# Half of the sums by source started while the rows are still being scattered

## The chip, the cores and the metric

One core of a Trainium2 chip runs the whole program. The metric is the device time of one execution in microseconds (us). The engines are PE (matrix products), DVE (vector), ACT (scalar), POOL (GpSimd, here it issues the indirect DMAs) and SP (SyncE, here it issues the plain DMAs). Each has its own queue and works through it in order; they wait for one another on semaphores.

## What is computed

Four graph layers over 3125 nodes of 128 features and 53125 edges sorted by destination. The part around the change is the first layer's sum of edge features by source and by destination:

```python
h = relu(layernorm(x))
edge_aggr = zeros(3125, 128)
edge_aggr = edge_aggr.at[row].add(edge_attr).at[col].add(edge_attr)   # row: source, col: destination
x = x + relu(concat([h, edge_aggr]) @ W1 + b1) @ W2 + b2
```

Layer 1 uses the sum by destination, layer 2 is a graph convolution over the same edges, layer 3 computes messages for each edge. All of them come after the stages told here.

## The kernel before

The edges are taken as 416 columns of 128 (EC). Four columns are a group (KC = 4, 104 groups), two are a pair (208 pairs, PG = 2 pairs a group). The nodes are 25 blocks of 128 (NB); source block b has its own region of 18 columns of rows in a DRAM table `rows_by_block` (CAP = 18 x 128 rows, the last block 9 columns), 129 words a row: the features and the node's number within its block.

**Scatter stage** (`place_and_count`). For each group g, PE computes with small matmuls the rank of every edge within its source block (`rank`, L895 to L905). DVE multiplies it with the block one-hots (`own_rank`, L834), reduces it to a place (L839) and casts it (L843); ACT copies the running count of each block as the base for the next group (`base_of_next`, L793). POOL then issues four indirect DMAs, each of which scatters one column of rows to its places (L769). SP loads the edge rows into a ring of eight groups. ACT writes the keys beside them (L779) and makes the low one-hots (`lows`, L786 and L789); DVE makes the wide one-hots (`hots`, L814 and L821), PE multiplies each pair (L921 to L930: a count of pairs of nodes, the sum by destination and the in-degree, into one of three PSUM bank pairs), and DVE adds the result to its window in SBUF (`collect`, L853 and L855), two pairs later. `rank` of group g+1 stands on PE ahead of the even pair of group g, and DVE's `which_block` (L828) for group g+2 waits for it, since the block one-hots are kept twice. Before each pair PE multiplies ones by ones (`stream_ones`, L384), three times, or 16 times in one of 32 pairs.

The order of each queue is the order of these loops. On ACT it is, for pair i: `lows(i)`, at the even pair the keys, at the odd pair `base_of_next(g+1)`, which waits for `own_rank(g+1)`. On DVE at the odd pair: `hots(i)`, `collect(i-2)`, `own_rank(g+1)`. On PE at the even pair: ones, `rank(g+1)`, pair; at the odd pair: ones, pair.

**Block sums** (`sum_blocks`). The table is read back block by block, in 74 reads of up to six columns (LR = 6) into four buffers (LB_IN = 4). DVE compares the keys of a read with 0 to 127 (L1125), PE sums the rows by these one-hots (L1181, float32: two matmul records for each column), and DVE adds the sum by destination (`add_dst`, L1117). Beside it ACT checks the counts of all 25 blocks in `between` (L1164), and DVE takes mean and variance of x. A small block then computes the flags that choose the fast path, and ends with 12 ones-matmuls; the dense layers follow.

Of the kernel before, what the change touches and what calls it, by code (L numbers as in the profile page):

```python
# [12 lines left out]
F32 = mybir.dt.float32  # L13
# [10 lines left out]
P = 128  # L24
# [57 lines left out]
LAST_BANK = 7  # L82
WARM_EVERY = 32


class Signal:
# [6 lines left out]
    def __init__(self, make, everywhere=False):  # L93
        self.make, self.everywhere, self.on_path, self.base = make, everywhere, {}, {}

    @property
    def h(self):
        branch = Signal.path is not None and not self.everywhere
        if branch not in self.on_path:
            self.on_path[branch] = self.make()  # L100
        return self.on_path[branch]
# [44 lines left out]
def build(nc, x, src, dst, ea, l0, l1, l2, l3, out):  # L146
    ctx = ExitStack()
    with ctx:
# [7 lines left out]
        def signal(name, everywhere=False):  # L156
# [3 lines left out]
            return Signal(make, everywhere)  # L160
# [98 lines left out]
        bounds = sb("bounds", [1, 2, NB])  # L259
        over = sb("over", [1, 2, NB])  # L260
# [22 lines left out]
        tab_row = sb("tab_row", [1, 2, 2, ST * P], I32)  # L283
        tab_bc = sb("tab_bc", [P, 2, 2, ST * P])

        shifts = [sb(f"shift{k}", [P, SLOTS_OF[k], GS[k]]) for k in range(2)]
# [15 lines left out]
        junk = grid_space.take([P, NP], U8)  # L302
        excess = grid_space.take([P, NB])
# [349 lines left out]
        pair_done = signal("pair_done")  # L653
        taken = signal("taken")
# [68 lines left out]
        def place_and_count():  # L723
# [15 lines left out]
            with nc.Block(no_gpsimd_drain=True) as block:  # L739
                @on(block.sync)  # L740
                def _(sp):
                    for g in range(ROWG, GROUPS):
# [6 lines left out]
                        if g == 6 * ROWG:  # L749
                            sp.wait_ge(vec.h, vec.at(1))  # L750
                            sp.dma_start(x_nm[:, 0:NB - 1, :], x[0:(NB - 1) * P, :].rearrange("(b p) f -> p b f", p=P)).then_inc(loaded.h, 16)
                            sp.dma_start(x_nm[0:NLAST, NB - 1, :], x[(NB - 1) * P:N, :]).then_inc(loaded.h, 16)
                    sp.wait_ge(loaded.h, loaded.at(16 * 23))
# [19 lines left out]
                def _(act):  # L773
# [24 lines left out]
                    for i in range(PAIRS):  # L798
# [4 lines left out]
                        if i % PG == 1 and g + 1 < GROUPS:  # L803
                            base_of_next(g + 1)

                @on(block.vector)
                def _(dve):
# [50 lines left out]

                    which_block(0)
                    which_block(1)  # L860
                    own_rank(0)
                    for i in range(PAIRS + 2):
# [11 lines left out]
                        if i % PG == 1 and g + 1 < GROUPS:  # L874
                            own_rank(g + 1)
# [1842 lines left out]
```

## Time and profile before

| | us |
|---|---|
| median of 3 runs (lowest to highest) | 1446.84 (1445.1 to 1453.07) |
| the profiled execution, its own time | 1445.09 |
| its span in the trace | 1443.2 |
| granted TensorE clock, mean | 0.971 of 2.4 GHz |
| scatter stage, first scatter to the first read of the block sums | 26.15 to 559.2 |
| block sums | 559.2 to 686 |

Times within the trace are counted from the start of the span. The profiled execution's own time is 1.9 us above its span. A busy time is that of instructions in work; what an engine waited for stands in brackets behind a row of the timeline.

### The profile page before, as it was taken

The numbers are of one execution on the slowest core, as the hardware profiler recorded it, in microseconds if no ns is written. First come the engines' busy times: TensorE is split into PE (matmuls) and PEld (weight loads), VectorE is DVE, ScalarE is ACT, GpSimd is POOL, SyncE is SP. The second block draws the span as 40 slices with busy tenths as digits, with TensorE's granted clock in tenths as the row PEclk, the third lists the DMA queues.
The fourth block names the chain that finished last, engine by engine and source line by source line (L and its number), as shares of the span: only waits on it lengthen the run. The fifth ranks groups of instructions, "written<-read, shape, count | busy, mean of one in ns | idle before, by whom it ended". The sixth has DMA issues, their size and how long they took to land. (4 is left out here: it accounts for less than half of the span.)

```text
span 1443.2 us, 32570 instructions
## 1 busy us (share of the span) xinstructions
PE 1243.0 (86%) x9643; PEld 908.2 (63%) x9644; DVE 881.1 (61%) x2785; ACT 555.4 (38%) x1465; POOL 809.5 (56%) x844
## 2 busy tenths in 40 slices
PE   5887888888888887898679998999999988898896
PEld 3554555555555555888459997477766766666665
DVE  6777878787877876766676537344444444444343
ACT  5444444444454446960222103333332222222222
POOL 5777777777777773000000000777777777777774
PEclk9999999999999999999889998899999999999997
DMA  7533335333333324877600001745555565555641
GB/s 230 137 106 104 104 105 148 102 105 104 106 104 106 107 72 138 237 246 217 30 18 2 2 1 52 203 133 153 156 154 155 161 159 150 152 140 145 149 111 42
DMA packets 198603, 174.73 MB, mean 121 GB/s; under 512 B 48820, under 2 KB 171174, under 8 KB 198342
## 3 DMA queue, kind: packets, MB, share of 16 engines
q1 hardware_dynamic: 171848, 118.36, 31.1%
q0 software_dynamic: 26624, 54.79, 12.9%
q8 instruction: 62, 1.02, 0.3%
q14 instruction: 69, 0.57, 0.2%
HBM read 134.89 MB, written 38.16 MB: 120 GB/s over the span
## 5 line engine op out<-in xcount | busy, mean ns | idle before, releaser
L2192 POOL DMA_INDIRECT between<-p_table,src_g x416 | 397.5, 956 | 472.5 <-DMA p_table<-n_nm 346.0
L384 PE MATMUL acc<-ones_b 128*128 128x512 bf16 x1603 | 425.5, 386 | 29.3 <-PEq L1407 15.5
L769 POOL DMA_INDIRECT rows_by_block<-h_t,mean_bc x312 | 300.6, 963 | 109.5 <-issue 77.1
L384 PEld LDWEIGHTS acc<-ones_b 128*128 128x128 bf16 x1603 | 142.5, 99 | 130.9 <-issue 39.2
L921 PE MATMUL acc<-n_nm 128*128 128x384 bf16 (+1 forms) x832 | 140.8, 291 | 87.2 <-DVE n_nm L821 86.4
L2302 ACT ACTIVATE between<-acc 128x256 f32<-128x256 f32 x208 | 79.9, 384 | 352.4 <-PE acc L2359 339.3
L853 DVE TENSOR_TENSOR between<-between,acc 128x600 f32 x208 | 161.3, 775 | 61.3 <-issue 51.7
L2391 PE MATMUL acc<-w_msg,between 128*128 128x128 f32 x832 | 184.1, 303 | 0.0
L2370 PEld LDWEIGHTS acc<-between 128*128 128x128 f32 x832 | 128.9, 197 | 71.4 <-issue 52.2
L2229 DVE TENSOR_TENSOR between<-acc,between 128x256 f32<-128x256 f32 x208 | 87.6, 421 | 139.9 <-DMA between<-p_table,src_g 90.0
L921 PEld LDWEIGHTS acc<-n_nm 128*128 128x128 bf16 x832 | 66.3, 97 | 164.0 <-DVE n_nm L821 134.8
L2370 PE MATMUL acc<-between 128*128 128x24 f32 x832 | 132.5, 240 | 42.4 <-DVE agg_sum L2269 40.7
L821 DVE TENSOR_SCALAR n_nm<-iota_w,agg_sum 128x600 bf16<-128x600 f16 x416 | 154.5, 412 | 0.0
L786 ACT ACTIVATE away<-iota_b,agg_sum 128x128 bf16<-128x128 bf16 x416 | 140.9, 385 | 0.0
L2391 PEld LDWEIGHTS acc<-w_msg,between 128*128 128x128 f32 x832 | 126.0, 191 | 1.7 <-issue 0.3
L793 ACT ACTIVATE bases<-acc 1x26 f32<-1x26 f32 x104 | 19.0, 182 | 265.7 <-DVE agg_sum L834 265.7
L1181 PE MATMUL acc<-n_nm,h_t 128*128 128x128 f32 x882 | 109.4, 280 | 11.5 <-DVE n_nm L1125 10.9
L769 POOL DMA_INDIRECT rows_by_block<-agg_sum,mean_bc x104 | 99.7, 959 | 32.5 <-issue 25.5
L2359 PE MATMUL acc<-ident,between 128*128 128x128 f32 x416 | 114.1, 275 | 0.0
L1181 PEld LDWEIGHTS acc<-n_nm,h_t 128*128 128x128 f32 x882 | 102.2, 191 | 18.8 <-DVE n_nm L1125 18.1
L789 ACT ACTIVATE n_nm<-away,ones 128x256 bf16<-128x256 bf16 x208 | 105.6, 508 | 6.8
L2269 DVE TENSOR_TENSOR agg_sum<-agg_sum,acc 128x24 f32 x208 | 37.4, 180 | 115.3 <-PE acc L2370 65.5
(204 smaller groups left out, 1950.4 us busy)
## 6 DMA issues: line engine op xcount, KB each, us to landing
h_t<-rows_by_block SPq DMA_DIRECT2D x73, 387.0 KB, 3.8
between<-in_edge_attr SPq DMA_DIRECT2D x207, 128.0 KB
h_t<-in_edge_attr SPq DMA_DIRECT2D x78, 256.0 KB, 3.2
between<-in_dst SPq DMA_DIRECT2D x51, 288.0 KB
between<-p_table,src_g POOLq DMA_INDIRECT x416
agg_sum<-in_edge_attr SPq DMA_DIRECT2D x25, 256.0 KB
rows_by_block<-h_t,mean_bc POOLq DMA_INDIRECT x312
rows_by_block<-x_nm SPq DMA_DIRECT2D x1, 4644.0 KB, 18.6
```

Source lines behind the costliest of these rows:

```text
L384: pe.matmul(acc[:, bank * BANK:(bank + 1) * BANK].rearrange("p (a n) -> p a n", n=P), ones_b[:, :], ones_b[:, :].rearrange("p (a n) -> p a ...
L769: pool.indirect_dma_start(rows_by_block, bass.IndirectOffsetOnAxis(ap=place_in_table[:, t:t + 1], axis=0), row_group(g)[:, j, :], None).th ...
L786: act.activation(away[:, h + j, :], iota_b[:, :], ACT.Abs, scale=-1.0, bias=lo_s[:, 2 * i + j:2 * i + j + 1])\
L789: act.activation(low_hot[:, h:h + 2, :], away[:, h:h + 2, :], ACT.Relu, scale=-1.0, bias=ones[:, 0:1]).then_inc(lows_made.h, 1)
L821: ins = dve.tensor_scalar(wide_hot[:, i % HOTB * 2 + j, :], iota_w[:, :], key_w[:, t:t + 1], None, ALU.is_equal)
L853: dve.tensor_tensor(between[:, :, bass.ds(first, W)], between[:, :, bass.ds(first, W)], acc[:, o:o + NB * WS].rearrange("p (b w) -> p b w" ...
L921: pe.matmul(acc[:, to:to + (b1 - b0) * WS].rearrange("p (b w) -> p b w", w=WS)[:, :, 0:W], low_hot[:, h + j, :], wide_hot[:, h + j, b0 * W ...
L1181: last = pe.matmul(acc[:, o:o + P], rows_in_block[:, q, j, 0:D], hot_in_block[:, q, j, :], start=is_first and j == 0, stop=is_last and j = ...
L2192: pool.indirect_dma_start(got[:, q, j * D:(j + 1) * D], None, p_table, bass.IndirectOffsetOnAxis(ap=src_g[:, n * G + j:n * G + j + 1], axi ...
L2359: last = pe.transpose(acc[:, o:o + P], rows[:, i, j, :], ident[:, :])
L2370: last = pe.matmul(acc[:, o:o + W], relued[:, i % MR, j, :], onehot[:, i * G + j, :], start=j == 0, stop=j == G - 1)
L2391: last = pe.matmul(acc[:, o:o + P], turned[:, i % MR, j * P:(j + 1) * P], w_msg[:, 2, :], start=False, stop=True)
```

## The change

A chunk is three columns (CT = 3) of a block's region. The new functions are `load_chunk`, `hots_of_chunk`, `sum_chunk` and `take_chunk`. 72 chunks, three for each of the 24 whole blocks, are summed within the scatter stage, in the order of the blocks, round by round. Chunk m is loaded by SP with group 32+m, its one-hots are made by DVE at the odd pair of group 29+m in one comparison, PE sums it at the odd pair of group 30+m in place of the three ones-matmuls and ahead of the pair itself, and ACT copies the sum out of PSUM into `home` at the odd pair of group 31+m. In the second and third round (m of 24 and more) PE first adds what is kept in `home` by a matmul with the identity. PE waits for the copy of the chunk before it. The ones-matmuls move behind `rank` and behind the wait for the pair's bank.

The block sums then read only what is left: nine columns of each block, in a read of six and one of three, 50 reads. DVE adds `home` and the sum by destination beforehand. x, whose memory the chunks use, is loaded here and no longer in the scatter stage. Of ACT's 25 checks 14 stay as they are, and the other 11 blocks are first united by DVE with ten bitwise ORs and checked in one. Counts kept at three points tell whether the chunks were full; if not, the general path is taken. The ones-matmuls before the block sums fall from 16 to 6, the 12 behind the flags go, and three are added before the first dense layer. Many signals of the general path now share a semaphore with others, which changes nothing on the fast one.

```diff
+ALONE = 14
 WARM_EVERY = 32
+CT = 3
+CROWS = CT * P
+CRING, CHOTS = 3, 3
+CHUNK_LOAD, CHUNK_HOT, CHUNK_SUM, CHUNK_TAKE = 32, 29, 30, 31
+CHUNKS = EC // KC - CHUNK_LOAD
+BY_CHUNK = [min(NB - 1, CHUNKS - c * (NB - 1)) for c in range(-(-CHUNKS // (NB - 1)))]
...
+                    def load_chunk(m):
+
+                        if m >= CRING:
+                            sp.wait_ge(chunk_summed.h, chunk_summed.at(m + 1 - CRING))
+                        row = m % (NB - 1) * CAP + m // (NB - 1) * CROWS
+                        sp.dma_start(chunk_rows[:, m % CRING, :, :], rows_by_block[row:row + CROWS, :].rearrange("(p j) w -> p j w", j=CT))\
+                          .then_inc(chunk_in[m % CRING].h, 16)
...
-                        if g == 6 * ROWG:
-                            sp.wait_ge(vec.h, vec.at(1))
...
+                        if g == CHUNK_LOAD:
+                            sp.wait_ge(tail_zero.h, tail_zero.at(32))
+                        if g >= CHUNK_LOAD:
+                            load_chunk(g - CHUNK_LOAD)
+                    sp.wait_ge(loaded.h, loaded.at(16 * 21))
...
+                    def take_chunk(m):
+                        act.wait_ge(chunk_summed.h, chunk_summed.at(m + 1))
+                        o, b = IDLE_BANK * BANK, m % (NB - 1)
+                        act.activation(home[:, b * P:b * P + P], acc[:, o:o + P], ACT.Copy).then_inc(chunk_taken.h, 1)
+
                     def base_of_next(g):
                         act.wait_ge(ranks_read.h, ranks_read.at(g + 1))
+                        c = (g - (CHUNK_LOAD - ROWG)) // (NB - 1)
+                        if g == CHUNK_LOAD - ROWG + c * (NB - 1) and 0 <= c < len(BY_CHUNK):
+                            act.activation(counts_at[:, c, :], acc[0:1, R_AT + RANKS:R_AT + RANKS + NB], ACT.Copy)
                         act.activation(bases[:, (g + 1) % 2, :], acc[0:1, R_AT + RANKS:R_AT + RANKS + NK], ACT.Copy).then_inc(based.h, 1)
...
                         if i % PG == 1 and g + 1 < GROUPS:
                             base_of_next(g + 1)
+                        if i % PG == 1 and 0 <= g - CHUNK_TAKE < CHUNKS:
+                            take_chunk(g - CHUNK_TAKE)
...
+                    def hots_of_chunk(m):
+                        dve.wait_ge(chunk_in[m % CRING].h, chunk_in[m % CRING].at(16 * (m // CRING + 1)))
+                        if m >= CHOTS:
+                            dve.wait_ge(chunk_summed.h, chunk_summed.at(m + 1 - CHOTS))
+                        dve.tensor_tensor(chunk_hot[:, m % CHOTS, :, :], iota[:, :].rearrange("p (a n) -> p a n", a=1).broadcast_to([P, CT, P]),
+                                          chunk_rows[:, m % CRING, :, D:KW].broadcast_to([P, CT, P]), ALU.is_equal).then_inc(chunk_hots.h, 1)
...
                         if i % PG == 1 and g + 1 < GROUPS:
                             own_rank(g + 1)
+                        if i % PG == 1 and 0 <= g - CHUNK_HOT < CHUNKS:
+                            hots_of_chunk(g - CHUNK_HOT)
...
+                    def sum_chunk(m):
+                        pe.wait_ge(chunk_hots.h, chunk_hots.at(m + 1))
+                        if m >= 1:
+                            pe.wait_ge(chunk_taken.h, chunk_taken.at(m))
+                        o = IDLE_BANK * BANK
+                        again = m >= NB - 1
+                        if again:
+                            b = m % (NB - 1)
+                            pe.matmul(acc[:, o:o + P], ident[:, :], home[:, b * P:b * P + P], start=True, stop=False)
+                        for j in range(CT):
+                            last = pe.matmul(acc[:, o:o + P], chunk_rows[:, m % CRING, j, 0:D], chunk_hot[:, m % CHOTS, j, :],
+                                             start=j == 0 and not again, stop=j == CT - 1)
+                        last.then_inc(chunk_summed.h, 1)
+
                     rank(0)
                     for i in range(PAIRS):
                         g, q, c = i // PG, i // PG % ROWG, i % PG * 2
-                        stream_ones(pe, IDLE_BANK, WARM_UP if i % WARM_EVERY == WARM_EVERY - 1 else WARM_PAIR)
                         if c == 0 and g + 1 < GROUPS:
                             rank(g + 1)
+                        if i >= PRING:
+
+                            pe.wait_ge(taken.h, taken.at(i + 1 - PRING))
+                        if c != 0 and 0 <= g - CHUNK_SUM < CHUNKS:
+                            sum_chunk(g - CHUNK_SUM)
+                        else:
+                            stream_ones(pe, at_bank(i) // BANK, WARM_UP if i % WARM_EVERY == WARM_EVERY - 2 else WARM_PAIR)
                         pe.wait_ge(hots_made.h, hots_made.at(i + 1))
...
-                for j in range(0, n, LR):
-                    reads.append((b, b * CAP + j * P, min(LR, n - j), j == 0, j + LR >= n))
+                done = CT * sum(b < k for k in BY_CHUNK)
+                for j in range(done, n, LR):
+                    reads.append((b, b * CAP + j * P, min(LR, n - j), j == done, j + LR >= n))
...
+                        if r == LB_IN:
+                            sp.wait_ge(vec.h, vec.at(1))
+                            sp.dma_start(x_nm[:, 0:NB - 1, :], x[0:(NB - 1) * P, :].rearrange("(b p) f -> p b f", p=P)).then_inc(loaded.h, 16)
+                            sp.dma_start(x_nm[0:NLAST, NB - 1, :], x[(NB - 1) * P:N, :]).then_inc(loaded.h, 16)
...
                     def add_dst(b):
                         dve.wait_ge(nodes_summed.h, nodes_summed.at(last_read[b] + 1))
                         o = b % 8 * BANK
-                        dve.tensor_tensor(agg_sum[:, b * P:b * P + P], acc[:, o:o + P], agg_dst[:, b * P:b * P + P], ALU.add).then_inc(agg_read.h, 1)
+                        dve.tensor_tensor(agg_sum[:, b * P:b * P + P], acc[:, o:o + P], home[:, b * P:b * P + P], ALU.add).then_inc(agg_read.h, 1)
...
                     for r in range(len(reads)):
                         where(r)
...
+                        if r == 2:
+                            dve.tensor_tensor(home[:, 0:(NB - 1) * P], home[:, 0:(NB - 1) * P], agg_dst[:, 0:(NB - 1) * P], ALU.add)
+                            dve.tensor_copy(home[:, (NB - 1) * P:NP], agg_dst[:, (NB - 1) * P:NP]).then_inc(homes.h, 1)
...
+                        b = r - 5 + ALONE
+                        if ALONE <= b < NB - 1:
+                            if b > ALONE:
+                                dve.wait_ge(united.h, united.at(b - ALONE))
+                            dve.tensor_tensor(union, between[:, ALONE, :].bitcast(I32) if b == ALONE else union, between[:, b + 1, :].bitcast(I32), ALU.bitwise_or)\
+                               .then_inc(united.h, 1)
+                        if r == STATS_FROM:
+                            dve.wait_ge(loaded.h, loaded.at(32))
+                        for b in range(2 * (r - STATS_FROM), min(2 * (r - STATS_FROM) + 2, NB)):
...
+                        while r >= 4 and done < reads[r - 2][0]:
                             add_dst(done)
...
-                    for b in range(NB):
-                        act.activation(junk[:, :], between[:, b, :], ACT.Relu, bias=low_bound[:, :], accum_out=excess[:, b:b + 1]).then_inc(checked.h, 1)
-                        if b < NB - 1:
+                    for b in range(ALONE + 1):
+                        if b == ALONE:
+                            act.wait_ge(united.h, united.at(NB - ALONE - 1))
+                        of = between[:, b, :] if b < ALONE else mean_bc[:, 2 * EC:2 * EC + NP // 4].bitcast(U8)
+                        act.activation(junk[:, :], of, ACT.Relu, bias=low_bound[:, :], accum_out=excess[:, b:b + 1]).then_inc(checked.h, 1)
+                        if b < ALONE:
...
-                    stream_ones(pe, LAST_BANK, WARM_UP)
+                    stream_ones(pe, LAST_BANK, WARM_SHORT // 2)
...
                 pe.matmul(acc[:, 3 * BANK:3 * BANK + D], w2_msg[:, :], w_upd[:, 1, :], start=True, stop=True).then_inc(upd_turned.h, 1)
-                stream_ones(pe, LAST_BANK, WARM_SHORT)
```

## Rows read from the trace of the kernel before

**Rows 1.** Head of the page.
```profile
span 1443.2 us, 32570 instructions
```

**Rows 2.** Timeline of POOL alone, first and last of the 416 scatters; start us, us.
```profile
26.15 1.16 POOL L769 DMA_INDIRECT rows_by_block<-h_t,mean_bc  x1 [11.20 <-ACT h_t L779]
...
556.33 0.96 POOL L769 DMA_INDIRECT rows_by_block<-agg_sum,mean_bc  x1 [0.30 <-issue]
```

**Rows 3.** Timeline, one group of the scatter stage, all engines.
```profile
300.31 0.27 DVE L828 TENSOR_TENSOR agg_sum<-iota,agg_sum 128x104 bf16<-128x104 f32 x1 [0.24 <-PE acc L905]
...
301.45 0.96 POOL L769 DMA_INDIRECT rows_by_block<-h_t,mean_bc  x1 [0.30 <-issue]
...
302.05 0.76 DVE L821 TENSOR_SCALAR n_nm<-iota_w,agg_sum 128x600 bf16<-128x600 f16 x2
...
302.86 0.44 PEld L921 LDWEIGHTS acc<-n_nm 128*128 128x128 bf16 x4 [1.44 <-DVE n_nm L821]
302.87 0.68 PE L921 MATMUL acc<-n_nm 128*128 128x384 bf16 x4 [0.95 <-DVE n_nm L821]
...
303.53 0.25 DVE L834 TENSOR_TENSOR agg_sum<-acc,agg_sum 128x104 f32<-128x104 f32 x1
...
303.82 0.81 PE L384 MATMUL acc<-ones_b 128*128 128x512 bf16 x3
303.82 0.18 ACT L793 ACTIVATE bases<-acc 1x26 f32<-1x26 f32 x1 [2.54 <-DVE agg_sum L834]
...
303.98 0.96 POOL L769 DMA_INDIRECT rows_by_block<-agg_sum,mean_bc  x1 [0.31 <-issue]
304.00 0.65 DVE L821 TENSOR_SCALAR n_nm<-iota_w,agg_sum 128x600 bf16<-128x600 f16 x2
...
304.56 0.48 PE L901 MATMUL acc<-bases,ones 1*128 1x130 f32 x2
...
305.37 0.27 DVE L828 TENSOR_TENSOR agg_sum<-iota,agg_sum 128x104 bf16<-128x104 f32 x1 [0.46 <-PE acc L905]
```

**Rows 4.** Waits, 200 to 500 us: in total us, times, longest.
```profile
ACT bases L793 <- DVE agg_sum L834: 152.6, 59, 4.3
```

**Rows 5.** Timeline, end of the block sums to the second dense layer.
```profile
681.68 2.94 PE L1181 MATMUL acc<-n_nm,h_t 128*128 128x128 f32 x24 [0.19 <-DVE n_nm L1125]
...
684.19 0.56 DVE L1125 TENSOR_TENSOR n_nm<-iota,h_t 128x384 f32<-128x384 f32 x1 [1.34 <-DMA h_t<-rows_by_block]
...
687.95 2.75 PE L384 MATMUL acc<-ones_b 128*128 128x512 bf16 x12
688.15 0.28 ACT L1225 ACTIVATE w_msg<-acc 128x128 f32<-128x128 f32 x1 [0.58 <-PE acc L1216]
...
700.53 0.60 PE L1373 MATMUL acc<-ident,n_nm 128*128 128x128 f32 x4
...
725.63 2.08 PE L1373 MATMUL acc<-ident,n_nm 128*128 128x128 f32 x8
```

**Rows 6.** The reads of the block sums, by their line.
```profile
L1106 SPq DMA_DIRECT2D h_t<-rows_by_block x74: 319/320/2813, 559.2 to 680.0; - x74
...
DMA to landing us min/median/max: 3.0/3.8/5.7
```

**Rows 7.** Groups by form, 559 to 735 us: count, busy us, mean ns, idle before.
```profile
L1125 DVE TENSOR_TENSOR n_nm<-iota,h_t 128x768 f32<-128x768 f32 x73 | 69.9, 957 | 40.4 <-DMA h_t<-rows_by_block 39.5
...
L1125 DVE TENSOR_TENSOR n_nm<-iota,h_t 128x384 f32<-128x384 f32 x1 | 0.6, 558 | 1.3 <-DMA h_t<-rows_by_block 1.3
...
L1225 ACT ACTIVATE w_msg<-acc 128x128 f32<-128x128 f32 x1 | 0.3, 277 | 0.6 <-PE acc L1216 0.6
```

**Rows 8.** Windows: busy us by engine, granted clock, DMA share, GB/s.
```profile
300.00:400.00 100.00, 82.52 (x658) 51.26 (x658) 78.39 (x244) 48.02 (x157) 75.24 (x79) 1.00 0.36 106
600.00:650.00 50.00, 46.62 (x372) 43.28 (x372) 34.56 (x72) 37.26 (x25) 0.00 (x0) 1.00 0.80 244
700.00:750.00 50.00, 35.62 (x188) 24.37 (x186) 37.07 (x154) 14.20 (x25) 0.00 (x0) 0.88 0.36 34
```

More of the change, by code:

```diff
@@ L99, in h @@
         if branch not in self.on_path:
-            self.on_path[branch] = self.make()
+            self.on_path[branch] = self.twin.h if branch and self.twin else self.make()
         return self.on_path[branch]
@@ L258, in build @@
         bases = sb("bases", [1, 2, NK])
-        bounds = sb("bounds", [1, 2, NB])
-        over = sb("over", [1, 2, NB])
+        chunk_space = Space(x_nm[:, :, :].rearrange("p b f -> p (b f)")[:, (CAP - FILLED) // P * KW if FILLED else 6 * KW:], F32)
+        chunk_rows = chunk_space.take([P, CRING, CT, KW])
+        chunk_hot = chunk_space.take([P, CHOTS, CT, P])
+        bounds = chunk_space.take([1, 2 + len(BY_CHUNK), NB])
+        over = chunk_space.take([1, 2 + len(BY_CHUNK), NB])
+        counts_at = chunk_space.take([1, len(BY_CHUNK), NB])
         low_bound = sb("low_bound", [P, 1])
@@ L653, in build @@
         pair_done = signal("pair_done")
+        chunk_in = [signal(f"chunk_in{q}") for q in range(CRING)]
+        chunk_hots = signal("chunk_hots")
+        chunk_summed = signal("chunk_summed")
+        chunk_taken = signal("chunk_taken")
         taken = signal("taken")
@@ L887, in _ @@
                     dve.tensor_tensor(over[:, 1, :], bases[:, GROUPS % 2, 0:NB], bounds[:, 1, :], ALU.is_gt)
+                    for c, n in enumerate(BY_CHUNK):
+                        dve.tensor_tensor(over[:, 2 + c, 0:n], counts_at[:, c, 0:n], bounds[:, 2 + c, 0:n], ALU.is_lt)
                 @on(block.tensor)
@@ L941, in place_and_count @@
             away_made.passed(EC)
-            loaded.passed(16 * 23)
+            for s in (chunk_hots, chunk_summed, chunk_taken):
+                s.passed(CHUNKS)
+            for q in range(CRING):
+                chunk_in[q].passed(16 * len(range(q, CHUNKS, CRING)))
+            loaded.passed(16 * 21)
             vec.passed(2)
@@ L1065, in build @@
         late = signal("late")
+        united = signal("united")
+        homes = signal("homes")
+        far_read = signal("far_read")
         def mean_and_variance(dve, b):
@@ L1126, in where @@
                                           rows_in_block[:, q, 0:k, D:KW].broadcast_to([P, k, P]), ALU.is_equal).then_inc(nodes_hot.h, 1)
+                    dve.tensor_reduce(odd[0:1, 3:4], over[:, :, :], AX.XY, ALU.add)
                     dve.scalar_tensor_tensor(pair_far[0:1, 0:PAIRS - RING].rearrange("p (a n) -> p a n", n=RING),
@@ L1188, in sum_blocks @@
             agg_read.passed(NB)
-            checked.passed(NB)
+            homes.passed(1)
+            far_read.passed(1)
+            loaded.passed(32)
+            checked.passed(ALONE + 1)
+            united.passed(NB - ALONE - 1)
             vec.passed(4)
@@ L1757, in node_tables @@
                 s.passed(k)
[L1760 to L1766 removed]
+        near = signal("near", twin=hot_used)
+        left = signal("left", twin=lo_hot)
+        mid = signal("mid", twin=lo_used)
+        far = signal("far", twin=cnt_ready)
+        z_made = signal("z_made", twin=evac)
+        z_scaled = signal("z_scaled", twin=rel_ready)
+        self_added = signal("self_added", twin=hot_ready)
         biased = signal("biased")
```

65 lines of the change are left out of this document (32 added, 33 removed).

## The prediction, as it went on record

> **What bounds the kernel now.** I read the page first: 1443.2 us of span [rows 1], PE the busiest engine. That says little, since much of its work is ones times ones, which only keeps it awake. So I went by stages. The change touches two: the scatter stage (to 559 us) and the block sums (559 to 686 us).
>
> Scatter stage. POOL issues 416 scatters, from 26.15 to 556.33 us [rows 2]: 530.2/415 = 1.28 us each, and in the steady part one every 1.265 us (two steps from 301.45 to 303.98 [rows 3]: 0.96 us of work and 0.30 us of issue). Four make a group, so POOL allows no group under 5.06 us. It hardly ever waits for more than that gap. POOL is the bound, and the other engines run at the same period: L828 starts at 300.31 and at 305.37 [rows 3], 5.06 us.
>
> The reader should now follow the second-longest thing, the loop that goes round once a group through DVE, ACT and PE [rows 3]: L828 (300.31) frees the block one-hots, DVE collects a pair (L853, L855), makes the odd pair's one-hots (L821), collects again, and reads the rank (L834, ends 303.78); ACT copies the base (L793, ends 304.00); PE may then rank the next group (L901 to L905, from 304.56), after which L828 starts again. Two things in it matter: PE starts the odd pair at 302.87, as soon as its one-hots are there and **before** L834 and L793; and ACT stands waiting for L834 in each group (152.6 us in 59 waits [rows 4]).
>
> Block sums. 74 reads, the first issued at 559.2 [rows 6], the last compared at 684.19 [rows 5]: 125.0/74 = 1.69 us each. DVE waits 39.5 us for their DMA [rows 7], whose engines are 80% busy at 244 GB/s [rows 8]. PE needs 24 records in 2.94 us [rows 5], 0.245 us a matmul (two records), 108 us for 441: DMA bounds, PE is just behind.
>
> **The change, part by part.**
>
> *The wait that is added.* Sum m runs on PE in group g = 30+m, ahead of the odd pair, and from m = 1 on waits for the copies 0 to m-1. Copy m-1 belongs to group 31+(m-1), the same g, and stands on ACT behind L793 of that group. L793 waits for L834, which DVE reaches only after both collections. So the odd pair, which started at 302.87, now waits for L834, L793, the copy and the sum; and behind it in PE's queue stands the rank of the next group, for which L828 waits. The loop closes through PE:
>
> - L828 start to L834 end: 303.78 - 300.31 = 3.47 us [rows 3]
> - to the end of L793: 0.22 [rows 3]
> - the copy 128x128 out of PSUM: 0.28, the same form at L1225 [rows 7]
> - hand over to PE: 0.03, an estimate: between the end of L834 and L793 lie 0.04 [rows 3]
> - the sum: 6 records of 0.1225 = 0.74 for m below 24; with the identity 8 records, 0.98; over the 71 that wait, (23x0.74+48x0.98)/71 = 0.90
> - the odd pair, L921 to the next instruction: 303.82 - 302.87 = 0.95 [rows 3]
> - the rank with its hand over, L901 to L828: 305.37 - 304.56 = 0.81 [rows 3]
>
> Sum 6.66 us, against 5.06. 71 groups x 1.60 = **+114 us**. POOL, with 5.06 us of work a group, stands idle in the rest: its bound is left.
>
> The Trainium skill ("TensorE: Matmul & The Clock Gate", "Step-by-step: what each phase is for") says that PE may pull a weight load ahead of running matmuls while matmuls keep their order. In the trace the load of the odd pair waited 1.44 us with its matmul [rows 3], so I take none of it. By the Trainium skill one load could leave the loop: at the 0.12 of a record, 71x0.12 = 9 us less.
>
> *The clock.* PE's work a group is 0.8 of rank, 0.8 of ones, two pairs of 0.95 and 0.90 of sum, 4.4 us in 6.66, or 66%, with one pause of over 2 us. In the scatter stage now it is 83% busy [rows 8] and the clock stays at 1.00; in a later stretch, at 71% busy and with long pauses, it was granted 0.88 [rows 8], that is 24% of the time at 1.2 GHz. At that level 8 records of L1373 took 2.08 us, against 4 in 0.60 at 2.4 GHz [rows 5]: 1.73 times. The 2.66 us of PE in the loop then cost 1.94 more, 8.60 us. With a fifth of the time there the mean is 1/(0.8/6.66+0.2/8.60) = 6.97 us: **+22 us**. Ends: 0 (the clock stays) and half the time, 7.51 us, +60.
>
> *The comparison on DVE.* 72 of 128x384: 0.56 us each [rows 7]. They stand behind L834, where DVE had 1.59 us to the next L828 and now has 3.2; hidden. Without that cover 72x0.56 = 40 us.
>
> *The ones.* They go behind the rank, so in groups without a sum the rank starts behind L793 and not behind the ones: up to the whole of DVE's idle before L828, 0.46 us in one group and 0.24 in the other [rows 3]. POOL holds groups 0 to 29 at 5.06, but the others may run ahead of it, and POOL catches up in the slow groups. 30x0.46 = 14 at most, 0 at least; between ends that no row decides I take the middle, **-6**. The Trainium skill ("SBUF — State Buffer", "Who interferes with whom") lets a two-port DVE operation and a POOL operation block each other wholly. The trace disagrees in part: two L821 took 0.65 us inside one POOL operation (304.00) and 0.76 in another place [rows 3]; a POOL that is often idle would by the Trainium skill's rule give those 0.11 back, 8 us over 71 groups; I count nothing for it.
>
> *Chunk loads.* 198 KB a group, over 6.66 us 30 GB/s on top of 106 at a DMA share of 0.36 [rows 8]; issued five groups ahead of their use. Hidden. SP's wait for a sum comes five groups before its rows are needed. Hidden too.
>
> *Block sums.* 216 of 441 columns are gone, 50 reads remain, 25 of six columns and 25 of three. By bytes 225/441x125 = 64 us, and the load of x (1.6 MB at 244 GB/s) 6.7: 71. By round trips of the four buffers: now 4x1.69 = 6.76; three-column reads save 0.40 of comparison, 0.73 of matmuls and up to 0.8 of landing (3.8 median, 3.0 least [rows 6]), 1.93, so (6.76+4.83)/2 = 5.8 on the mean, 50x5.8/4 = 72, with x 79. DVE's own work: the comparisons fall to 25x0.96+25x0.56 = 38; ten unions of 800 words and the homes of 3072 come in, by the 0.96 of 768 elements 10x1.0+4x0.96 = 14 [rows 7]; the rest is now 34.6 busy in 50 us less 28.3 of comparisons [rows 8], 6.3, so 16 in 125. Together 68. ACT's checks fall from 25 to 15. I take 77 for 125: **-48**. Ends: -61 (bytes alone), -34 (50 reads at 1.69, and x).
>
> *The twelve ones behind the flags* end at 690.70; without them L1225, over at 688.43, is the last of its block [rows 5]: **-2**. The three ones in the first dense block lie beside DVE's L1367. Other edits (bounds, counts, signals shared by the two paths): under 1 us.
>
> Sum: +114+22-6-48-2 = +80 on the profiled execution's 1445.1 us, **1525 us**. (The median of the runs is 1.7 us above that execution; I leave it.)
>
> **Rivals.**
>
> 1. *The copy is never late* (faster). PE would not wait if copy m-1 were done when it has finished the even pair, that is 0.70+0.95 = 1.65 us after the rank; by the rows it is done 0.03+3.47+0.22+0.28 = 4.0 us after. It decides from the point where the loop is under 5.06 us: then POOL stays the bound and only the second stage counts, 1445-48-2 = 1395 us. For it speaks POOL's tight cadence; against it the order on ACT. Chance 0.07.
> 2. *The comparison sets the pace* (faster, little): the loop does not close, but each group grows by the uncovered 0.56: 1445+40-50 = 1435. Against: DVE is 78% busy now [rows 8], 4.0 us, and 4.5 is still under 5.06. Chance 0.03.
> 3. *The loop closes and the block sums do not shrink*, because DVE's extra work and small reads hold them: 1445+114+22-6 = 1575, or more with the clock at half. Against: none of the four sums above is over 79. Chance 0.04.
> 4. *The loop closes and the clock stays full*: 1445+114-6-48-2 = 1503. It is part of the forecast's 0.85, about 0.2 of it. (With the load pulled ahead as the Trainium skill has it, 1494.)
> 5. *The early sums don't take place*: if a block had fewer than 384, 768 or 1152 rows by its round, the general path would run. A block gets about 20 of 512 rows a group, 500 by group 24; no row prices that path. Chance 0.01.
>
> **Numbers.** Forecast 0.85 (1525, its clock part included), rivals as above. What can be told from no change is about 0.5%, 7 us. Slower 0.88, same 0.02, faster 0.10. The bounds together give 1445+114-13-14-61-2 = 1469 and 1445+114+60-34-0 = 1585; all ends at once are unlikely, so 1482 to 1570, which leaves out some 2 in 10, rivals 1 to 3 among them.
>
> **What would show it.** Right: in the changed kernel's scatter stage, groups from the 31st on 6.5 to 7.5 us apart, PE waiting over 2 us a group for ACT's copy, POOL idle some 1.6 us a group, a granted clock under 1.00 there; the last scatter near 685 us; reads over in 71 to 85 us. Wrong: POOL still at one in 1.265 us throughout; or the copy starting before L834 of its group; or the clock nearer 0.5, which would put the time over 1570.

## The result, and the profile after

The changed kernel took 1529.99 us (median of 4 runs, 1523.0 to 1536.02), the kernel before 1446.32 beside it: ratio 1.0584 [1.0558, 1.0611], 5.8% slower. Forecast: 1525 us, range 1482 to 1570. The profiled execution after took 1527.85 us.

New line numbers: L795 is the scatter; L827 the base (L793 before); L870 the reading of the rank (L834); L864 the block one-hots (L828); L879 the placing's conversion (L843); L820 the copy of a sum; L965 and L967 the sum's identity and its three matmuls; L988 to L997 a pair; L951 to L955 the rank; L1207 the comparison of the block sums (L1125). The head of the page, and its rows of the scatter and the base (busy us, mean ns | idle before, and what ended most of it):

```profile
span 1526.0 us, 32581 instructions
...
PEclk9999868779899889998998999979999999999996
...
L795 POOL DMA_INDIRECT rows_by_block<-h_t,mean_bc x312 | 302.9, 971 | 203.5 <-ACT h_t L805 90.1
...
L827 ACT ACTIVATE bases<-acc 1x26 f32<-1x26 f32 x104 | 18.9, 182 | 363.2 <-DVE agg_sum L870 363.2
```

GpSimd (POOL) does the work of before, but now waits 203.5 us ahead of three quarters of its scatters: it has ceased to be the bound. Timeline of one group of the scatter stage after, to set against [rows 3]:

```profile
513.79 0.67 PE L988 MATMUL acc<-n_nm 128*128 128x384 bf16 x4
...
514.45 0.96 POOL L795 DMA_INDIRECT rows_by_block<-h_t,mean_bc  x1 [2.20 <-ACT h_t L805]
...
514.81 0.48 PE L951 MATMUL acc<-bases,ones 1*128 1x130 f32 x2
...
515.62 0.27 DVE L864 TENSOR_TENSOR agg_sum<-iota,agg_sum 128x104 bf16<-128x104 f32 x1 [2.00 <-PE acc L955]
...
518.82 0.25 DVE L870 TENSOR_TENSOR agg_sum<-acc,agg_sum 128x104 f32<-128x104 f32 x1
519.00 0.54 DVE L899 TENSOR_TENSOR x_nm<-iota,x_nm 128x384 f32<-128x384 f32 x1
519.11 0.18 ACT L827 ACTIVATE bases<-acc 1x26 f32<-1x26 f32 x1 [4.32 <-DVE agg_sum L870]
519.20 0.25 ACT L820 ACTIVATE home<-acc 128x128 f32<-128x128 f32 x1
...
519.59 0.46 PE L965 MATMUL acc<-home,ident 128*128 128x128 f32 x2 [2.43 <-DVE x_nm L899]
...
519.89 0.83 PE L967 MATMUL acc<-x_nm 128*128 128x128 f32 x6
...
520.56 0.67 PE L988 MATMUL acc<-n_nm 128*128 128x384 bf16 x4
```

The reader can go round the loop here: rank (514.81), L864 (515.62), L870 (518.82), L827, the copy L820 until 519.45, and only then the sum (519.59), for which PE stood idle 2.43 us, and the odd pair (520.56), 6.77 us behind its predecessor (513.79). The view names L899 as the releaser; the sum doesn't read those one-hots (they are made a group ahead), so I read it as the copy, and the runs below test that. Windows after, columns as in [rows 8]; the last three are single rounds, from the start of one rank to the next:

```profile
60.00:160.00 100.00, 92.05 (x739) 62.02 (x737) 83.90 (x274) 53.83 (x177) 75.94 (x80) 1.00 0.37 108
188.00:226.00 38.00, 32.06 (x181) 23.88 (x180) 20.84 (x67) 13.09 (x45) 29.01 (x30) 0.63 0.45 121
250.00:600.00 350.00, 257.06 (x1888) 198.61 (x1889) 207.64 (x670) 130.25 (x451) 189.81 (x196) 0.87 0.35 103
361.91:368.46 6.55, 4.33 (x41) 3.48 (x38) 3.99 (x13) 2.62 (x10) 4.11 (x5) 1.00 0.37 111
368.46:375.23 6.77, 4.34 (x42) 3.50 (x39) 4.45 (x14) 2.62 (x10) 3.66 (x5) 1.00 0.36 107
530.09:538.84 8.75, 7.99 (x41) 6.04 (x38) 3.99 (x13) 2.62 (x9) 4.11 (x5) 0.50 0.26 76
```

POOL issues 80 scatters in the first 100 us, its full cadence, and from 250 us on 196 in 350 us, one in 1.79 us; the clock has fallen from 1.00 to 0.87. A round with the identity takes 6.55 or 6.77 us at the full clock and 8.75 at 0.50 (1.2 GHz). Where the time went is read off L879 (L843), once a group, here groups 31 and 102, after:

```profile
165.53 0.15 DVE L879 CAST mean_bc<-place_f 128x4 int32<-128x4 f32 x1
...
667.85 0.16 DVE L879 CAST mean_bc<-place_f 128x4 int32<-128x4 f32 x1
```

and before:

```profile
181.06 0.32 DVE L843 CAST mean_bc<-place_f 128x4 int32<-128x4 f32 x1
...
545.96 0.15 DVE L843 CAST mean_bc<-place_f 128x4 int32<-128x4 f32 x1
```

- Group 31 comes 181.06 - 165.53 = 15.5 us **earlier**.
- The 71 groups after it take 502.3 us, 7.08 each, against 364.9, 5.14 each: **+137.4**.
- The last scatter starts at 677.89, against 556.33 [rows 2]: +121.6 in all.
- Block sums, first to last comparison (the line's source view gives first and last start):

```profile
L1207 DVE TENSOR_TENSOR n_nm<-iota,h_t x50: 543/750/960, 683.8 to 766.8; 128x768 f32<-128x768 f32 x25, 128x384 f32<-128x384 f32 x25
```

83.0 us, against 562.3 to 684.2, 121.9, in the same view of before: **-38.9**. Sum +82.7; the spans differ by 82.8. All the rest of the program nets to 0.1.

### The profile page after: what moved, and what is told of

The parts are those of the page before. It is cut to its first block and busy times, and to the rows that moved or that the text cites. A ratio compares the mean times of both kernels' runs of the same rounds, so it can differ in the third digit from the quotient of the medians.

```text
span 1526.0 us, 32581 instructions
## 1 busy us (share of the span) xinstructions
PE 1261.5 (83%) x9504; PEld 968.4 (63%) x9505; DVE 865.1 (57%) x2852; ACT 536.0 (35%) x1520; POOL 814.1 (53%) x844
## 3 DMA queue, kind: packets, MB, share of 16 engines
q8 instruction: 62, 1.02, 0.3%
## 5 line engine op out<-in xcount | busy, mean ns | idle before, releaser
L795 POOL DMA_INDIRECT rows_by_block<-h_t,mean_bc x312 | 302.9, 971 | 203.5 <-ACT h_t L805 90.1
L398 PE MATMUL acc<-ones_b 128*128 128x512 bf16 x1368 | 377.7, 400 | 37.4 <-PEq L1511 15.0
L398 PEld LDWEIGHTS acc<-ones_b 128*128 128x128 bf16 x1368 | 129.7, 101 | 133.3 <-issue 44.1
L2474 PE MATMUL acc<-between 128*128 128x24 f32 x832 | 132.8, 241 | 39.8 <-DVE agg_sum L2373 38.9
L988 PE MATMUL acc<-n_nm 128*128 128x384 bf16 (+1 forms) x832 | 158.7, 319 | 0.0
L827 ACT ACTIVATE bases<-acc 1x26 f32<-1x26 f32 x104 | 18.9, 182 | 363.2 <-DVE agg_sum L870 363.2
L857 DVE TENSOR_SCALAR n_nm<-iota_w,agg_sum 128x600 bf16<-128x600 f16 x416 | 143.6, 386 | 0.0
L988 PEld LDWEIGHTS acc<-n_nm 128*128 128x128 bf16 x832 | 87.9, 107 | 74.8 <-issue 24.7
L795 POOL DMA_INDIRECT rows_by_block<-agg_sum,mean_bc x104 | 101.2, 973 | 56.2 <-issue 27.2
L864 DVE TENSOR_TENSOR agg_sum<-iota,agg_sum 128x104 bf16<-128x104 f32 x104 | 27.6, 266 | 172.7 <-PE acc L955 169.4
L965 PE MATMUL acc<-home,ident 128*128 128x128 f32 x96 | 24.8, 344 | 96.5 <-DVE x_nm L899 94.0
## 6 DMA issues: line engine op xcount, KB each, us to landing
x_nm<-rows_by_block SPq DMA_DIRECT2D x72, 193.5 KB, 2.5
```

The source lines that it names most:

```text
L398: pe.matmul(acc[:, bank * BANK:(bank + 1) * BANK].rearrange("p (a n) -> p a n", n=P), ones_b[:, :], ones_b[:, :].rearrange("p (a n) -> p a ...
L795: pool.indirect_dma_start(rows_by_block, bass.IndirectOffsetOnAxis(ap=place_in_table[:, t:t + 1], axis=0), row_group(g)[:, j, :], None).th ...
L857: ins = dve.tensor_scalar(wide_hot[:, i % HOTB * 2 + j, :], iota_w[:, :], key_w[:, t:t + 1], None, ALU.is_equal)
L988: pe.matmul(acc[:, to:to + (b1 - b0) * WS].rearrange("p (b w) -> p b w", w=WS)[:, :, 0:W], low_hot[:, h + j, :], wide_hot[:, h + j, b0 * W ...
L2474: last = pe.matmul(acc[:, o:o + W], relued[:, i % MR, j, :], onehot[:, i * G + j, :], start=j == 0, stop=j == G - 1)
```

## The experiments

All twelve ran on four other chips (two to four kernels on each), and there the kernel before itself takes 1822 to 1853 us (medians) instead of 1446. So ratios below hold for those chips, and what carries over is read from the traces; the times that were expected for a chip like the first could not be tested. The kernel before was therefore profiled there too; it comes first.

**The kernel before on such a chip.** No edit.

> The kernel before itself, profiled on the chip of the two runs beside it, to see whether its own scatter stage shows the pauses. If the pauses belong to the chip and not to the change: groups 31 to 102 some 6.4 to 6.8 us apart on the mean instead of 5.1, with GpSimd idle beyond its 0.30 us in a third to a half of the groups, a span near 1820 us, and the block sums (DMA only, no GpSimd) as in the first profile of the kernel before, 125 us from first read to last comparison. If the pauses came with the edits: a scatter stage of 530 us.

1832.8 us (one run). Windows and the waits of 250 to 600 us:

```profile
250.00:600.00 350.00, 264.49 (x1678) 158.09 (x1679) 189.94 (x622) 122.96 (x400) 192.52 (x200) 0.78 0.27 81
```

```profile
POOL rows_by_block L769 <- ACT h_t L779: 72.2, 21, 7.2
...
DVE agg_sum L828 <- remote: 63.4, 12, 9.1
```

It issues 200 scatters in 350 us here. DVE stops up to 9.1 us ahead of L828, released by nothing that the profile shows, and POOL runs dry behind it. In one stop, from 337.39 to 344.35, the rank that L828 waits for is over at 337.75, so that wait does not explain it. Groups 31 to 102 are 6.97 us apart (6.4 to 6.8 expected), the quickest quarter under 5.48. The block sums are untouched (120.8 us, first to last comparison), and from a clock of 1.00 it is down to 0.78. The pauses came without the change: the first alternative of the expectation.

**The changed kernel there.**

> The changed kernel itself, beside the two edits below on the same chip. Theory of the prediction: about 1530 us where the kernel before takes 1446 (ratio 1.058); the group period of the scatter loop alternates 7.03 and 6.29 us at the full clock, and TensorE waits for ScalarE's copy 36 to 48 times. Rival, that the loop is paced by something common to both kernels (as in the four kernels measured first, whose kernel before took some 1825 us): ratio 0.97 to 1.00.

1836.26 us, ratio 0.9923 [0.9864, 0.9983]: not slower here. But from 250 to 600 us its scatter stage is the one seen above, nearly to the row:

```profile
250.00:600.00 350.00, 258.94 (x1857) 197.90 (x1857) 205.81 (x662) 128.37 (x443) 189.63 (x197) 0.85 0.35 103
```

197 scatters against 196, PE busy 258.94 against 257.06. Its first 31 groups, ahead of any sum, are not: 6.81 us each, where they took 4.53 on the first chip. The stops are there before the slow loop begins, and all but end with it. The waits from 250 to 600 us show it, beside the row of the kernel before above (total us, times, longest): first the changed kernel, then the kernel with the copy first and the one with the sum ahead of the even pair, both told below:

```profile
DVE agg_sum L864 <- remote: 4.3, 1, 4.3
DVE agg_sum L864 <- remote: 69.8, 14, 9.0
DVE agg_sum L864 <- remote: 71.3, 17, 8.1
```

All twelve traces agree. Before group 31 each has 9 to 12 such stops of over 1 us. From there on the kernels with a quick loop have 18 to 26, and those that keep the slow one (the changed kernel, the two runs with eight ones, the one with one matmul) 1 to 3. Idle time ahead of it that the view puts to no wait at all is 23.8 us in the changed kernel for 6.9 to 9.1 in these others, which does not make up for it. So the changed kernel pays little for the stops in its slow part, and the kernel before pays throughout; why a slower loop has so few stays open. Both stages stand at 7.0 to 7.2 us a group here, the last scatter starts at 758.21, some 20 us behind the 738.45 of the kernel before (on another of these chips) instead of 121.6, and the 39 us of the block sums outweigh it. The rival's ratio came out. Its mechanism did so in part: the stops pace the kernel before and the early groups of both, but behind them the changed kernel goes at its own 6.6 to 6.8 us a round at the full clock.

**The copy ahead of the base.** ScalarE's queue alone is changed:

```
                         if i % PG == 1 and 0 <= g - CHUNK_TAKE < CHUNKS:
                             take_chunk(g - CHUNK_TAKE)
+                        if i % PG == 1 and g + 1 < GROUPS:
+                            base_of_next(g + 1)
```

(and the same two lines of base_of_next taken out ahead of it.) Run three times, on three chips.

> The changed kernel with one thing swapped: on ACT the copy of a chunk's sum stands ahead of the copy of the base, so it no longer waits for DVE's rank. All work is the same. If the loop through ACT sets the period (my theory), groups with a chunk fall from 7.07 us to POOL's 5.06, PE waits no more for the copy, the clock stays at 1.00 in the scatter stage, and the whole takes 1400 to 1415 us: 1445, less the 38 that the block sums gained, less about 2. If instead the work that was added (DVE's comparison, the chunk loads, PE's sum) sets the period, it stays near 7 us and the time above 1515. If the copy is only half of it, something between, 1430 to 1500, with the wait moved to another line.

> The same kernel as e1 (the copy of a chunk's sum ahead of the copy of the base on ACT), meant for a chip on which the kernel before takes about 1445 us. On the chip of e1 to e4 it took 1828, with pauses of 2.2 us in a queue between instructions that no wait explains, so that POOL was not the bound there. My theory: the period of the groups with a chunk is POOL's 5.06, the clock is 1.00 there, 1400 to 1415 us. Rival (the added work sets the period): above 1515. Between, 1430 to 1500, if half of the wait moves elsewhere.

> ScalarE copies the chunk's sum ahead of the base of the next group's ranks. Theory (the copy that stands behind VectorE's last rank comparison costs every second group 0.7 us and the pause in which the clock falls): 71 groups get 0.3 to 0.7 us shorter at the full clock, and the clock falls less; 25 to 70 us less than the changed kernel on the same chip. Rival (the wait is only moved to the rank's base): within 10 us of the changed kernel.

1794.76 us, ratio 0.9838 [0.9751, 0.9925]; 1801.54, 0.9881 [0.9786, 0.9976]; 1836.36, 0.9922 [0.9862, 0.9982], this one on the chip of the changed kernel and level with it. A gain of 25 to 70 us was expected of the last, none was measured, so the rival's number came out (within 10 us), though not its mechanism: PE does not wait for the rank's base instead. In the trace the copy's wait is gone nevertheless. PE's waits ahead of L965 (total us, times): the view of the changed kernel on the same chip has the first row, that of the last of these three has the second and names no copy:

```profile
  ACT home L820: 53.1, 23
  DVE by_dst L891: 150.9, 48
```

One group of the last, undisturbed:

```profile
533.58 0.27 DVE L864 TENSOR_TENSOR agg_sum<-iota,agg_sum 128x104 bf16<-128x104 f32 x1 [0.38 <-PE acc L955]
...
534.19 0.26 ACT L820 ACTIVATE home<-acc 128x128 f32<-128x128 f32 x1
...
535.08 0.20 DVE L891 TENSOR_TENSOR by_dst<-by_dst,acc 128x48 f32 x1
535.33 0.49 PE L965 MATMUL acc<-home,ident 128*128 128x128 f32 x2 [0.81 <-DVE by_dst L891]
...
538.75 0.27 DVE L864 TENSOR_TENSOR agg_sum<-iota,agg_sum 128x104 bf16<-128x104 f32 x1 [0.65 <-PE acc L955]
```

The copy ends at 534.45, and PE waits 0.81 us for the next thing that is late, DVE's collection (L891), whose bank the pair needs. L864 to L864 is 5.17 us, near POOL's 5.06. It is no single case: of the 71 rounds, rank to rank, 26, 22 and 23 are under 5.2 us in these three traces, none in the changed kernel on the last of these chips and one on the first. So the order on ScalarE did set the changed kernel's period; on these chips the stops come back with the quick loop and take the gain (14 of the 71 groups last over 9 us in the last, 3 in the changed kernel).

**Eight ones in PE's pause**, ahead of the sum: `stream_ones(pe, at_bank(i) // BANK, 8)` before `sum_chunk`. Run twice.

> The changed kernel with eight ones-matmuls more on PE ahead of the wait for the copy, in the 72 groups with a chunk: 1.7 us of work at the full clock inside a pause of about 2.4 us. The wait and the loop stay. If the clock's share was as I read it (27% of the scatter stage at 1.2 GHz, period 7.07 against 6.66), the clock now stays at 1.00 there and the period is 6.66: 71x0.41 = 29 us less, about 1500. If the clock costs nothing here, the time stays at 1530. If the ones are themselves in the way, it is over 1530.

> The same kernel as e2 (eight ones-matmuls more on PE ahead of the wait for the copy), on a chip as in e5. With the loop as before and the clock kept at 1.00: period 6.66 against 7.07, about 29 us less than the changed kernel, 1500. If the clock costs nothing: 1530. If the ones are in the way: over 1530.

1792.48 us, ratio 0.9835 [0.977, 0.9899]; 1794.88, 0.9859 [0.9773, 0.9944]. The window of the first:

```profile
250.00:600.00 350.00, 328.52 (x2395) 218.31 (x2394) 217.88 (x702) 136.80 (x473) 201.96 (x209) 1.00 0.38 109
```

The clock is held at 1.00, and 209 scatters are issued for the changed kernel's 197 on another of these chips, 196 on the first: 6.70 us a group for 7.11. Filling the wait shortens nothing in the loop (the quickest quarter of the groups ends at 6.29 us, in the changed kernel at 6.35). The difference of 0.41 us a group, 29 us over 71, is taken between chips, and one kernel (the copy first) moves by 0.49 a group from chip to chip, so it alone proves little. The first chip's own trace says the same: there 42 of the 71 rounds, from sum to sum, are wholly at the full clock and take 6.65 us on the mean, and all 71 take 7.11.

**The ones moved, and nothing else**, in the kernel before:

> The kernel before with one part of the change alone: the ones-matmuls stand behind the rank and behind the wait for the pair's bank, and write that bank; no chunks. DVE and PE should then go round in about 4.5 us instead of 5.06, as the first 30 groups of the changed kernel did, and run ahead of POOL until the ring of rows holds them. If POOL's 1.265 us for each of 416 scatters is the bound, the time is that of the kernel before within 0.3%, 1442 to 1450, and the last scatter starts at 555 to 558 us. If the loop of DVE and PE was the bound, the scatter stage takes 104x4.5 us and the time falls to about 1390.

1834.74 us, ratio 1.0039 [1.0005, 1.0072]: no gain from the order of the ones alone, and the interval allows a loss of up to 0.7%. The loop itself is quicker: of the rounds wholly at the full clock, rank to rank from group 31 on, the median is 4.54 us (4.88 in the trace of the kernel before on another of these chips). But with the stops in it the mean is 6.6, so this run does not tell whether POOL was the bound on the first chip, as it was meant to.

**One matmul a chunk**, no identity (only a third of a chunk's rows is summed, and the kept sum isn't added): `again = False`, `for j in range(1)`.

> The changed kernel, where each chunk's sum on PE is one matmul in place of three, and the matmul with the identity that adds the kept sum is left out (two thirds of the chunk rows and the kept sums are not summed); waits, loads, comparison and copies stay. If the sum lies on the loop, 23 groups lose 0.49 us and 48 lose 0.73, 46 us in all: 1484, up to 15 more if the longer pause lowers the clock. If the sum is hidden behind something else, the time stays near 1530.

1802.06 us, ratio 0.9879 [0.9809, 0.995]. 205 scatters in 350 us with the clock at 0.70:

```profile
250.00:600.00 350.00, 284.12 (x1665) 201.84 (x1666) 213.51 (x689) 133.67 (x461) 200.91 (x205) 0.70 0.38 107
```

The quickest quarter falls only from 6.35 to 6.16 us, where 0.49 or 0.73 us of sum were left out, but those quarters mix two clocks. Single rounds, rank to rank, part them:

```profile
687.15:693.06 5.91, 3.67 (x36) 2.82 (x33) 3.99 (x13) 1.77 (x8) 2.95 (x3) 1.00 0.44 125
589.29:596.79 7.50, 6.71 (x36) 4.76 (x33) 4.02 (x13) 2.62 (x9) 4.11 (x5) 0.50 0.34 100
```

At the full clock 5.91 us stand against 6.55 and 6.77 (mean 6.66), 0.75 less: the sum lies on the loop in full. What takes most of the gain back is the clock: only 5 of these 71 rounds are wholly at the full one, 43 in the changed kernel on the first chip. The wait stays (2.24 us ahead of L967 in the round at the full clock).

**The sum ahead of the even pair.** The sum stands where the ones of the even pair stood, right behind the rank, and its copy is one group earlier:

```
-CHUNK_LOAD, CHUNK_HOT, CHUNK_SUM, CHUNK_TAKE = 32, 29, 30, 31
+CHUNK_LOAD, CHUNK_HOT, CHUNK_SUM, CHUNK_TAKE = 32, 29, 30, 30
-                        if c != 0 and 0 <= g - CHUNK_SUM < CHUNKS:
+                        if c == 0 and 0 <= g - CHUNK_SUM < CHUNKS:
```

> The sum stands in the place of the ones ahead of the group's even pair, right behind the rank, and its copy is taken one group earlier, behind the base that the rank needs; ones stay ahead of the odd pair. Theory (the whole loss is the wait of the odd pair for a copy that stands behind the last comparison of its own group): the copy is done before the rank that stands ahead of the sum, TensorE never waits for it by over 0.2 us, the loop is that of the kernel before, and the time is that of the kernel before less the 38 to 40 us of the block sums: some 1405 us where the kernel before takes 1446, 1780 to 1800 where it takes 1825 to 1850, ratio 0.96 to 0.985. Rival (the sum's work itself, the comparison or the loads of the chunks cost the time): groups 6.6 to 7.0 us apart at the full clock still, and a ratio as the changed kernel's, 0.992 or more.

1803.47 us, ratio 0.9878 [0.9821, 0.9936]: between the two expectations (0.985 at most, 0.992 at least), so the trace decides. A group of it:

```profile
444.32 0.48 PE L951 MATMUL acc<-bases,ones 1*128 1x130 f32 x2
...
444.93 0.45 PE L965 MATMUL acc<-home,ident 128*128 128x128 f32 x2
...
445.49 0.96 POOL L795 DMA_INDIRECT rows_by_block<-h_t,mean_bc  x1 [0.30 <-issue]
...
448.19 0.26 DVE L870 TENSOR_TENSOR agg_sum<-acc,agg_sum 128x104 f32<-128x104 f32 x1
...
448.48 0.18 ACT L827 ACTIVATE bases<-acc 1x26 f32<-1x26 f32 x1 [3.66 <-DVE agg_sum L870]
448.57 0.25 ACT L820 ACTIVATE home<-acc 128x128 f32<-128x128 f32 x1
448.81 0.46 PE L951 MATMUL acc<-bases,ones 1*128 1x130 f32 x2 [0.17 <-issue]
```

PE never stands idle ahead of L965 (its source view lists no wait; ahead of L967 it lists none for a copy), the loop takes 448.81 - 444.32 = 4.49 us, under POOL's 5.06, and POOL issues with its bare 0.30 between. The comparison, the loads and the matmuls of all 72 chunks are still there, so none of them was the cost by being done; it was the place of the sum. Its last scatter starts at 738.73, in the kernel before on the same chip at 738.45. That they agree so closely is luck, since the same scatter stage in the next kernel ends at 731.82; no loss is seen there, and the block sums keep their gain (81.4 us).

**x in nine pieces**, three blocks to each of eight reads, in place of one load ahead of a read; first on the kernel with the copy first, then on the last one.

> The same, and x's load in the block sums cut into nine, spread over eight reads. Theory (the one load stands ahead of the next block read and costs the 6.97 us wait at 692 us): 4 to 7 us less than the kernel with only the copy first. Rival (the bytes have to be moved at some time in a stage paced by its reads): within 2 us of it.

> The same with the load of x in nine pieces. Expected 5 to 6 us less than the run beside it: the first to the last comparison of the block sums took 77.8 us with the pieces and 83.0 to 83.3 without, in the three runs before. Rival: a new wait elsewhere takes it back, within 2 us.

1816.55 us, ratio 0.9816 [0.9751, 0.9882], and 1791.29, 0.9836 [0.9772, 0.9899]; the intervals overlap those of the runs beside them (0.9922, 0.9878), so the traces decide. First to last comparison is 77.9 us against 83.3, and 76.1 against 81.4: 5.3 to 5.4 us (80.8 to 84.6 in all runs with one load of x). What goes is this wait of the profile after, behind the one load of x; no wait ahead of a comparison is over 2.8 us with the pieces, and with the one load the longest is 6.15 to 7.21:

```profile
689.17 3.64 SPq L1188 DMA_DIRECT2D x_nm<-in_x  x1
...
692.86 3.38 SPq L1184 DMA_DIRECT2D h_t<-rows_by_block  x4
...
699.09 0.56 DVE L1207 TENSOR_TENSOR n_nm<-iota,h_t 128x384 f32<-128x384 f32 x1 [6.97 <-DMA h_t<-rows_by_block]
```

## Why the prediction was right, step by step

- **The wait that is added: right.** +114 and +22 us for the loop and its clock were forecast, +137.4 measured. The loop closes through the copy: with the copy out of it, it goes round in 5.17 or 4.49 us, with it in 6.77 in the group shown. The sum of [rows 3] gave 6.66; at the full clock the rounds take 6.65 on the mean (from conversion to conversion they alternate between some 6.3 and 7.0). Term by term, the group shown against the forecast: L864 to the end of L870 3.45 us for 3.47, to the end of L827 0.22 for 0.22, the copy 0.16 behind that for 0.28 (it starts before L827 is over), hand over 0.14 for 0.03, the sum 0.97 for 0.98, the pair 1.02 for 0.95, the rank 0.81 for 0.81. PE waits at the sum in 67 of 72 cases, 1.93 us on the mean: some 0.8 at the low clock, mostly 2.2 to 2.4 at the full one. Neither the rival of a late comparison nor that of a copy in time took place.
- **The clock: right in size.** 7.08 us a group was measured for 6.97 forecast. Its price is 0.41 us a group by the eight ones and 0.45 by the first chip's own rounds, 29 to 32 us for 22. A round at the low clock took 8.75 us where 8.60 was forecast. It came in stretches: 188 to 226 us at 0.63, with PE 84% busy, right behind the first waits.
- **The rule on the early weight load** (the Trainium skill, "TensorE: Matmul & The Clock Gate", "Step-by-step: what each phase is for") was worth an estimated 0.12 us of the loop. The pair's loads do start early, within the sum's matmuls (519.89 to 520.72):

```profile
520.45 0.54 PEld L988 LDWEIGHTS acc<-n_nm 128*128 128x128 bf16 x4
```

  But from the sum's start to the pair's lie 520.56 - 519.59 = 0.97 us, of 0.98 forecast, and from the pair's start to the rank's 514.81 - 513.79 = 1.02, no less than the 0.95 of [rows 3]: the loop gains nothing by it.
- **The rule on the shared port** (the Trainium skill, "SBUF — State Buffer", "Who interferes with whom") was worth an estimated 8 us with an idle POOL. In the profile's group of the wide one-hots (L857, L821 before) one takes 386 ns after and 412 before, over 416, 11 us of DVE's own time; only those of the odd pair lie in the loop, and no run here separates them.
- **The early groups: mis-sized.** -6 forecast, -15.5 measured, past the end of 14 that I had named. DVE and PE ran (165.53 - 25.1)/31 = 4.53 us a group there, not 5.06; the kernel with the ones moved and no sums goes round in 4.54 too. POOL was not faster for it, it worked the lead off later: in the window from 188 to 226 us it issues 30 scatters in 38 us at full cadence, while the clock is at 0.63. That the ones moved alone would bring nothing on the first chip, since without a slower loop behind it the lead is never used, is argued and not shown: it ran where the stops set the pace.
- **The block sums: mis-sized.** -48 forecast (77 us), -38.9 measured. From the first read's issue at 680.8 to the start of the last comparison, 766.8, it is 86.0 us, 9 more than forecast. The load of x was put at 7 us and stopped the reads for 6.97. What was too low is the price of a read: (86.0 - 7.0)/50 = 1.58 us, where the mean of full and half reads had been put at 1.45, 7 us over 50; the other 2 are those by which 77 was taken for the 79 of that way of counting. Half reads hardly come quicker than full ones did (1.69); what holds them is not separated.
- **Errors cancel, and that is luck:** 9.5 us more from the early groups, 9 less from the block sums. Loop and clock together were right to 2 us, but this too is a difference: 7.08 us a group for 6.97 is 7 us more, and the kernel before took 5.14 in the same groups for the 5.06 that was subtracted, 6 us. The -13 in the sum of the lower bound (1469) is worked out nowhere in the prediction.
- **The twelve ones behind the flags (-2): right.** From the last comparison to the first instruction of the dense layers (L1471, L1367 before) it is 5.65 us in each trace with the change and 7.40 in each without: -1.75. It does not show in the total, as the stretches behind it are longer by as much. The other small edits were not tried by themselves.

**What stays open.** What stops DVE on the four chips: the stops come ahead of L828 or L864, with no releaser, not in the block sums, and hardly where the loop is slow. And the time of the kernel with the sum ahead of the even pair and x in pieces on a chip like the first. From rows it would be 1445 - 39 - 5 = 1401 us, an estimate: its loop is under POOL's cadence, and 39 and 5 are measured (the 5 on the other chips). What was measured is that it is 1.6% faster than the kernel before where that one takes 1830 us. Two places in PSUM for alternate sums, so that a sum need not wait for the copy of the one before, were not tried either.

## What to carry to other kernels

A piece of work that fits into idle time can still cost its whole latency, if it waits for something that stands late in another queue of the same round: go round the loop and add it up before counting busy shares. Then ask for the place in the round at which the needed copy has already been made for another reason; here a condition and a constant, changed, took the round from 6.55 or 6.77 us to 4.49 in the group shown, under the 5.06 of POOL. And a kernel bound by one queue and one bound by a slow loop may change places on a chip with other pauses (ratio 1.058 on one, 0.992 on another): compare them on both.

## What the runs showed of the hardware

- Four chips ran the unchanged kernel 26 to 28% slower (1822 to 1853 us for 1446), with stops of DVE up to 9.1 us and a mean clock of 0.84 for 0.97; the block sums, whose transfers SP issues, took the same (120.8 us for 121.9). The four traces with the slow loop had 1 to 3 of these stops from group 31 on, those with a quick loop 18 to 26.
- A load of 1.6 MB ahead of reads of 387 and 193.5 KB held them up 6.97 us; in nine pieces it costs 5.3 to 5.4 us less.
- The clock fell to 0.87 in a loop that left PE idle 2.2 to 2.4 us in its rounds at the full clock, of 6.55 or 6.77 us, with PE 73% busy over 350 us; it stayed at 1.00 with eight ones more in each pause, at 94%. At the low level the same round took 8.75 us.
